# First layer of a two-layer kernel: the next chunk's score table is made from 26 rows on TensorE and six steps on VectorE

## What is computed

```python
def _L0_attn_ref(feature, wq_w, wq_b, w2_w, w2_b, ln_g, ln_b):
    q_local = feature @ wq_w + wq_b
    init_buf = feature[:, :W, :]                      # W = 64
    def step(buf, q_i):
        ki = concatenate([buf, zeros((B, 1, D))], axis=1)
        scores = einsum('bwd,d->bw', q_i[:, None, :] * ki, w2_w) + w2_b[0]
        alpha = softmax(scores, axis=1)
        v_i = einsum('bwd,bw->bd', ki, alpha)
        new_buf = concatenate([buf[:, 1:, :], v_i[:, None, :]], axis=1)
        return (new_buf, v_i)
    _, vs = lax.scan(step, init_buf, qs)              # 960 steps, one after the other
    v_local = concatenate([feature[:, :W, :], vs])
    y = tanh(v_local) * feature + feature
    return layer_norm(y, ln_g, ln_b)
x = L0_attn_feature
x = x + _layernorm(_L0_attn_ref(_layernorm(x), ...))
x = x + _layernorm(_L0_ffn_ref(_layernorm(x), ...))
```

## Time and profile before

| | |
|---|---|
| median of three runs | 2723.62 us |
| the profiled execution | 2731.38 us |
| its span | 2729.3 us |
| VectorE (DVE) busy | 2157.0 us, 79% of the span, 15955 instructions |
| ScalarE (ACT) busy | 1340.9 us, 49% |
| TensorE matmul (PE) busy | 1172.4 us, 43% |
| GpSimd (POOL) busy | 451.5 us, 17% |
| VectorE by slices of a fortieth of the span | 6999999999999999999947898866776666865233 |
| TensorE by slices | 2011010101010110101026777878877777778696 |

### The profile page before, as it was taken

How to read it: one execution, slowest core, us unless ns; L and a number is a source line. 1 busy time by engine, 2 the same in 40 slices (tenths; PEclk the granted TensorE clock), 3 DMA queues, 4 the chain that set the end, 5 groups by cost and what they waited for, 6 DMA issues and landing times. The chain is left out here.

```text
span 2729.3 us, 41936 instructions
## 1 busy us (share of the span) xinstructions
PE 1172.4 (43%) x7272; PEld 522.0 (19%) x7272; DVE 2157.0 (79%) x15955; ACT 1340.9 (49%) x3573; POOL 451.5 (17%) x1053
## 2 busy tenths in 40 slices
PE   2011010101010110101026777878877777778696
PEld 1000000000000000000011111224322333233365
DVE  6999999999999999999947898866776666865233
ACT  2343434444444434343322555658755775578642
POOL 0111111111111111111000110141024111311211
PEclk8555555555555555555566999889988988789898
DMA  5000000000000000000032031003120311001100
GB/s 144 1 4 3 5 3 5 4 4 5 3 5 3 5 3 5 3 5 5 2 79 39 1 78 32 13 16 100 24 46 19 89 44 33 22 19 35 34 1 24
DMA packets 82322, 65.85 MB, mean 24 GB/s; under 512 B 11838, under 2 KB 66920, under 8 KB 82056
## 3 DMA queue, kind: packets, MB, share of 16 engines
q1 hardware_dynamic: 78984, 56.89, 8.7%
q0 software_dynamic: 3072, 6.30, 0.7%
HBM read 34.77 MB, written 28.05 MB: 23 GB/s over the span
## 5 line engine op out<-in xcount | busy, mean ns | idle before, releaser
L1470 DVE TENSOR_REDUCE nm_half<-pair 128x2 f32<-128x1024 f32 x512 | 611.4, 1220 | 197.8 <-PE pair L1718 183.0
L342 ACT ACTIVATE ex<-row,nmax 128x65 f32<-128x65 f32 x960 | 336.1, 350 | 769.2 <-DVE row L408 676.7
L1358 ACT ACTIVATE pt<-pair 128x1024 f32<-128x1024 f32 x512 | 513.3, 1025 | 379.3 <-PE pair L1728 365.2
L403 DVE SCALAR_TENSOR_TENSOR junk<-ex,tab 128x65 f32<-128x65 f32 x2850 | 581.2, 229 | 1.9 <-issue 0.9
L523 PE MATMUL p_s<-tab,bdg 128*128 128x32 f32 x120 | 31.9, 406 | 769.2 <-DVE tab L408 769.2
L408 DVE SCALAR_TENSOR_TENSOR tab<-rz,raw 128x1 f32<-128x1 f32 (+1 forms) x1890 | 297.8, 158 | 10.9 <-ACT ex L342 5.5
L1694 PE MATMUL p_o<-pt,va 128*9 128x512 f32 x2048 | 296.1, 653 | 7.0 <-ACT pt L1358 7.0
L420 DVE STREAM_SHUFFLE row<-tab 128x130 f32<-128x130 f32 x930 | 274.8, 295 | 2.3 <-issue 2.1
L1718 PE MATMUL pair<-ks,qs 48*128 48x512 bf16 x1024 | 209.0, 419 | 112.8 <-ACT pt L1358 56.1
L403 DVE DVE_READ_ACCUMULATOR junk<-ex,tab 128x1 f32 x2850 | 233.1, 82 | 0.2
L1728 PE MATMUL pair<-qs,ks 50*128 50x512 bf16 x1024 | 210.1, 414 | 53.1 <-ACT pt L1358 23.8
(11 more groups left out here) (281 smaller groups left out, 2216.0 us busy)
## 6 DMA issues: line engine op xcount, KB each, us to landing
parts_dram<-parts SPq DMA_DIRECT2D x48, 256.0 KB, 3.5
qs<-parts_dram SPq DMA_DIRECT2D x32, 192.0 KB, 4.8
ks<-parts_dram SPq DMA_DIRECT2D x32, 192.0 KB, 5.3
hid<-xs_dram SPq DMA_DIRECT2D x33, 128.0 KB, 2.1
ys_dram<-hid SPq DMA_DIRECT2D x33, 128.0 KB, 1.8
x<-in_x SPq DMA_DIRECT2D x4, 512.0 KB, 8.5
w_W<-in_W SPq DMA_DIRECT2D x1, 2048.0 KB
w_W<-in_W SPq DMA_DIRECT2D x8, 256.0 KB
```

Source lines behind the costliest of these rows:

```text
L342: nc.scalar.activation(ex[:, r % 2, :], row[:, r % 2, 1, :], ACT.Exp, bias=nmax[:, r % 2:r % 2 + 1], accum_out=z[:, r % 2:r % 2 + 1]).then ...
L403: nc.vector.scalar_tensor_tensor(junk[:, g, :], ex[:, k, :], CAP, tab[:, g, r:r + ROW], ALU.min, ALU.mult, accum_out=raw[:, g:g + 1]).then ...
L1358: nc.scalar.activation(pt[:, kt % 2, :, tokens(t)], pair[fill.pair][:, :, :], ACT.Exp, scale=SCALE).then_inc(s_exp, 1)
L1470: nc.vector.reduce_max(nm_half[:, t, hp % 2, :, q], pair[fill.pair][:, :, :], AX.X, negate=True)\
```

## The change

`tab`'s plane 0 becomes a tensor of its own, `tab0`, with two buffers for alternate chunks and FORE = 6 more columns in front. The coefficients `tab` get two buffers too. `ex`, `z` and `rz` have four buffers instead of two, `junk` and `raw` one slot more.

In chunk c, TensorE makes the table of chunk c + 1 from the coefficients of the first FROM = 26 rows, in row 26, and no longer after row 31. VectorE reads it at the end of row 27 (`next_table`). The scores of the next chunk's queries against the last six vectors are made on VectorE as those vectors' weights come: six products over the exponentials of rows 26 to 31 (`next_products`), each followed by a division into the next column (`next_score`), placed in rows 28 to 31. Row 31 then makes the first new score of the next chunk, and rows 30 and 31 make the broadcasts for rows 0 and 1 of the next chunk, so that its row 0 follows as any other row. Only 30 rows of a chunk (SHORT) make a column of scores for the own chunk. GpSimd fills the new columns with b0 and clears the coefficients of the other buffer, behind its three copies. ScalarE's work between rows moves by one or two rows: `vr` from row 1 to 3, `vt1` from 4 to 6, `bdg` from 8-11 to 9-12, most parts of the layer norms by one row. Once, in the preparation, 16 copies of the identity are made instead of 8.

The core of the diff:

```diff
+FORE = 6
+FROM = L - FORE
+SHORT = L - 2
...
                 nc.gpsimd.tensor_copy(qn[:, :], qt[:, c + 3, :]).then_inc(s_qn, 1)
+                if c:
+                    pool.wait_ge(s_bdc, c + 1)
+                    nc.gpsimd.memset(tab[:, (c + 1) % 2, :, WIN:], 0.0).then_inc(s_clear, 1)
+                nc.gpsimd.tensor_copy(tab0[:, (c + 1) % 2, WIN:], b0_row[:, :]).then_inc(s_fill, 1)
                 applied(c)
...
-                    if r:
+                    if c or r:
                         act.sem_inc(s_pace_act, 1)
-                        act.wait_ge(s_new, (L - 1) * c + r)
...
-                    if r == 1:
+                    if r == 3:
                         act.wait_ge(s_vall, c + 1)
...
+            def products(slot, n, other, done):
+
+                nc.vector.scalar_tensor_tensor(junk[:, slot, :], ex[:, n % 4, :], CAP, other, ALU.min, ALU.mult,
+                                               accum_out=raw[:, slot:slot + 1]).then_inc(done, 1)
...
+            def next_table(c):
+
+                dve.wait_ge(s_scores, c + 2)
+                nc.vector.tensor_scalar(tab0[:, (c + 1) % 2, 0:WIN], p_s[:, 0:WIN], b0[:, :], None, ALU.add)\
+                    .then_inc(s_table, 1)
+
+            def next_products(c, i):
+
+                if i == 0:
+                    dve.wait_ge(s_fill, c + 1)
+                    dve.sem_inc(s_pace, 1)
+                    dve.wait_ge(s_table, c + 3)
+                else:
+                    dve.wait_ge(s_next, FORE * c + i)
+                products(4, FROM + i, tab0[:, (c + 1) % 2, i:i + ROW], s_raw_next)
+
+            def next_score(c, i):
+                dve.wait_ge(s_raw_next, FORE * c + i + 1)
+                divided(tab0[:, (c + 1) % 2, WIN + i:ROW + i].unsqueeze(2), 4, 5, FROM + i, s_next)
...
             for c in range(NC):
-                nc.vector.tensor_copy(tab[:, 0, WIN:], b0_row[:, :]).then_inc(s_table, 1)
-                dve.wait_ge(s_scores, c + 1)
-                nc.vector.tensor_scalar(tab[:, 0, 0:WIN], p_s[:, 0:WIN], b0[:, :], None, ALU.add).then_inc(s_table, 1)
-                dve.wait_ge(s_table, 2 * (c + 1))
-                dve.sem_inc(s_pace, 1)
-
-                nc.vector.stream_shuffle(row[:, 0, 1, :], tab[:, 0, 0:ROW], [0] * L).then_inc(s_row, 1)
-                shifted(1, 0)
-                dve.wait_ge(s_row, L * c + 1)
-                nc.vector.reduce_max(nmax[:, 0:1], row[:, 0, 1, :], AX.X, negate=True).then_inc(s_max, 1)
-                dve.wait_ge(s_bdc, c + 1)
-                nc.vector.memset(tab[:, 1:3, WIN:], 0.0).then_inc(s_clear, 1)
-                dve.wait_ge(s_clear, c + 1)
+                more = c < NC - 1
                 for r in range(L):
...
                     dve.wait_ge(s_exp, n + 1)
-                    if r:
-                        coefficients(c, r - 1)
...
+                    if n:
+                        coefficients(n - 1)
+                    nc.vector.reciprocal(rz[:, n % 4:n % 4 + 1], z[:, n % 4:n % 4 + 1]).then_inc(s_rz, 1)
+                    if more and r == L - 3:
+                        next_products(c, 1)
+                    if not final:
                         dve.wait_ge(s_row, n + 2)
...
+                        products(3, n, row[:, (n + 1) % 2, 0, :], s_raw_new)
+                    if more and r == L - 2:
+                        next_score(c, 3)
+                    if more and r == L - 1:
+                        next_products(c, 5)
+                    if r < SHORT:
+                        products(0, n, tab0[:, c % 2, FORE + r:FORE + r + ROW], s_raw_score)
+                    if not final:
+                        largest(n + 1)
+                    if more and r == L - 2:
+                        next_products(c, 4)
+                    if not final:
+                        dve.wait_ge(s_raw_new, n + 1)
                         dve.sem_inc(s_pace, 1)
                         dve.wait_ge(s_rz, n + 1)
...
+                        divided(row[:, (n + 1) % 2, 1, WIN - 1:WIN].unsqueeze(2), 3, 4, n, s_new)
+                    if more and r == L - 3:
+                        next_score(c, 1)
+                    if more and r == L - 1:
+                        next_score(c, 5)
+                    if r < SHORT:
                         dve.wait_ge(s_raw_score, m)
...
+                        divided(tab0[:, c % 2, FORE + r + WIN:FORE + r + ROW].unsqueeze(2), 0, 1, n, s_score)
+                    if more and r == L - 4:
+                        next_products(c, 0)
+                    if more and r == L - 3:
+                        next_products(c, 2)
+                    if c and not r:
+                        dve.wait_ge(s_clear, c - 1)
+                        dve.sem_inc(s_pace, 1)
+                    if n:
                         dve.wait_ge(s_coef, n)
...
+                    products(1, n, tab[:, c % 2, 0, r:r + ROW], s_raw)
+                    if more and r == L - 2:
+                        next_score(c, 4)
+                    products(2, n, tab[:, c % 2, 1, r:r + ROW], s_raw)
+                    if more and r == L - 3:
+                        next_score(c, 2)
+                    if r < SHORT:
                         dve.wait_ge(s_score, m)
                         dve.sem_inc(s_pace, 1)
...
+                        shuffled(n + 2, c, r + 2, FORE + r + 1)
+                    elif more:
+                        dve.wait_ge(s_next, FORE * c + FORE - L + 1 + r)
+                        dve.sem_inc(s_pace, 1)
+                        shuffled(n + 2, c + 1, r + 2 - L, FORE + r + 1 - L)
+                    if more and r == FROM + 1:
+                        next_table(c)
+                    if more and r == L - 4:
+                        next_score(c, 0)
+                    if more and r == L - 3:
+                        next_products(c, 3)
...
-                    nc.tensor.matmul(p_s[q, 0:L], qn[:, q], vt1[:, q], start=True, stop=True)
-                pe.wait_ge(s_coef, L * (c + 1))
+                    nc.tensor.matmul(p_s[q, 0:FORE], qn[:, q], vt2[:, L * b + FROM:L * b + L], start=True, stop=True)
+                    nc.tensor.matmul(p_s[q, FORE:FORE + L], qn[:, q], vt1[:, q], start=True, stop=True)
+                pe.wait_ge(s_coef, L * c + FROM)
                 for g in range(2):
-                    ins = nc.tensor.matmul(p_s[:, L:WIN], bdg[:, g, :], tab[:, 1 + g, WIN:], start=g == 0, stop=g == 1)
+                    ins = nc.tensor.matmul(p_s[:, FORE + L:WIN], bdg[:, g, :], tab[:, c % 2, g, WIN:WIN + FROM],
+                                           start=g == 0, stop=g == 1)
```

More of the change, by code:

```diff
@@ L70, in window_attention @@
         b0 = sb("b0", [P, 1])
-        b0_row = sb("b0_row", [P, L])
-        zero_row = sb("zero_row", [P, L])
+        b0_row = sb("b0_row", [P, FORE + L])
+        zero_row = sb("zero_row", [P, FORE + L])
         stats = sb("stats", [P, NK, 6])
@@ L85, in window_attention @@
         bdc = sb("bdc", [P, 2, P])
-        tab = sb("tab", [P, 3, WIN + L])
+        tab0 = sb("tab0", [P, 2, FORE + WIN + L])
+        tab = sb("tab", [P, 2, 2, WIN + L])
         row = sb("row", [P, 2, 2, ROW])
         nmax = sb("nmax", [P, 2])
[L91 to L95, removed]
+        ex = sb("ex", [P, 4, ROW])
+        z = sb("z", [P, 4])
+        rz = sb("rz", [P, 4])
+        junk = sb("junk", [P, 5, ROW])
+        raw = sb("raw", [P, 5])
         g_row, b_row = xt["g_row"], xt["b_row"]
@@ L395, in _ @@
                 q = slice(L * b, L * b + L)
-                for g in range(2):
-                    nc.vector.tensor_copy(tab[q, 1 + g, L * g:L * g + L], ident[q, q]).then_inc(s_init, 1)
-            dve.wait_ge(s_init, 14)
+                for u in range(2):
+                    for g in range(2):
+                        nc.vector.tensor_copy(tab[q, u, g, L * g:L * g + L], ident[q, q]).then_inc(s_init, 1)
+            dve.wait_ge(s_init, 22)
             dve.wait_ge(s_mask, 3)
-            def weighted(g, k, r, done):
-                nc.vector.scalar_tensor_tensor(junk[:, g, :], ex[:, k, :], CAP, tab[:, g, r:r + ROW], ALU.min,
-                                               ALU.mult, accum_out=raw[:, g:g + 1]).then_inc(done, 1)
@@ L419, in shifted, with shuffled @@
+            def shuffled(m, c, q, start):
+                src = tab0[:, c % 2, start:start + ROW]
                 pair = bass.AP(src.tensor, src.offset, [src.ap[0], [1, 2], [1, ROW]])
[L420 to L424, removed]
+                nc.vector.stream_shuffle(row[:, m % 2, :, :], pair, [q] * L).then_inc(s_row, 1)
@@ new lines, in _ @@
+            nc.vector.tensor_copy(tab0[:, 0, WIN:], b0_row[:, :]).then_inc(s_table, 1)
+            dve.wait_ge(s_table, 1)
+            dve.sem_inc(s_pace, 1)
+            dve.wait_ge(s_scores, 1)
+            nc.vector.tensor_scalar(tab0[:, 0, FORE:FORE + WIN], p_s[:, 0:WIN], b0[:, :], None, ALU.add)\
+                .then_inc(s_table, 1)
+            dve.wait_ge(s_table, 2)
+            dve.sem_inc(s_pace, 1)
```

(12 more changed lines are left out.)

65 lines of the change are left out of this document (29 added, 36 removed).

## The result

The changed kernel took 2694.68 us (median of four runs, 2690.15 to 2697.54) against 2724.23 us of the kernel before (four runs): ratio 0.989, 95% interval 0.987 to 0.991. Forecast were 2708 and a range from 2695 to 2722. The direction was right; the gain was -29.5 us where -15.6 was forecast, and the time lay 0.3 us under the range.

A forecast was written before the change was run, and what follows sets the result against it. VectorE and its loop through ScalarE's exponential were taken to bound the first layer, with 3.45 us per chunk boundary. Terms summed to -0.57 per boundary, -16.5 us over 29, -15.6 with preparation and last chunk: 2708 us, range 2695 to 2722.

The forecast's parts named there:

- item 1: Chunk boundary: the 3.45 us between row 31 and the next chunk's row 0 goes, -3.45 per boundary.
- item 2: Row 31 becomes an ordinary row that also makes the next chunk's first new score, +1.24 us per boundary.
- item 4: End of row 27: VectorE's read of the table moves there, without waiting for TensorE, +0.11 us per boundary.
- rival D: Matmuls come late for row 27's read or ScalarE's p_v copy, so the boundary only moves: 2724 us, chance 0.03.
- rival C: Look-ahead products and scores in rows 28 to 31 run serially, +1.40 us per boundary: 2748 us, chance 0.07.
- item 6: Row 0: GpSimd's two bdc tile products now run beside VectorE's busy row, +0.55 us per boundary, bounds 0.32 and 0.86.
- item 5: Copy of b0_row and clearing of tab move from VectorE to GpSimd, +0.08 us per boundary.
- item 7: More instructions mean more unexplained VectorE stalls, and the boundary hid its share: +0.05 us per boundary.
- items 2 to 4: Row 31 made ordinary, +1.24; six look-ahead products and scores, +0.85; table read moved to row 27, +0.11 us.
- Rival B: Contention falls where VectorE waits anyway; bdc costs 0.32, row 29's stall and extra fetches nothing: 2698 us, chance 0.22.
- Rival A: In row 0 bdc blocks VectorE for its whole 0.86 us; moved GpSimd operations cost 0.15: 2719 us, chance 0.2.
- the rule that spoke against the change: VectorE instructions with two SBUF inputs contend with GpSimd reads, the loser fully blocks; bdc's full length could be lost.

The follow-up runs named there:

- the second profile: Profile of the changed kernel, run again unchanged; its rows took 1293.2 us, against 1317.2 for the kernel before, also run again.
- the memsets: Changed kernel with eight further 128x128 GpSimd memsets per chunk, ahead of bdc: sum of row medians 42.50 us, against 42.40 without.
- the repeated run: The changed kernel once more, unchanged: 2698.25 us against 2722.51 for the kernel before, ratio 0.991.

## Why the prediction was off

The path was right: the boundary went whole (item 1), row 31 became an ordinary row (item 2), the table is there in time (item 4, rival D), the look-ahead doesn't run serially (rival C: one stall of 0.06 and one of 0.11), and the moved waits cost nothing. What failed is the size of terms of the sum, item 6 above all: bdc in row 0 was priced at 0.55 by the earlier trace rows and costs 0.39. Items 5 and 7, priced at +0.08 and +0.05, cost nothing.

| per boundary, us | forecast | measured | |
|---|---|---|---|
| items 2 to 4, rows 27 to 31 over four ordinary rows and one new | 0.96 | 1.03 | an unforeseen stall of the broadcast in row 30 |
| item 6, bdc in row 0 | 0.55 | 0.39 | shown by giving it to ScalarE |
| item 5, the moved GpSimd work | +0.08 | -0.02 | rows 1 to 7, 1.38 over ordinary rows before, 1.36 after (1.37 in the second profile) |
| item 7, stalls without a cause | +0.05 | -0.02 | mean less median: 0.85 before, 0.84 after (0.83) |
| sum with items 1 and 2 | -0.57 | -0.83 | the mean period fell by 0.90, and by 0.84 between the second profiles |

Of the 0.26, bdc is 0.16. It was taken from a pair of operations with a gap between them (starts 0.53 apart) for a pair without one (0.86 in all), whose second operation holds the one-column step for 0.12 less, as the starts and ends above show. Item 5 is 0.10: the clearing costs nothing, by the memsets, and the copy that fills the new columns cost nothing of its own either: in chunk 10 it ends at 494.61, and the coefficient step that starts at 494.58 is held until 495.04 by the layer norm's first operation, which held a product for as long before (0.30). Item 7 is 0.07; it was a guess at what is hidden in the boundary. Against these stand 0.07 too little for items 2 to 4. What the first pair's 0.90 has beyond that is mostly an ordinary row of 1.238 instead of 1.240 in the first profile of the changed kernel, 28 times a chunk; in its second the row is 1.240 again.

Rival B is nearest, and was held for the less likely, but it isn't the case that came. It had bdc at 0.32 and no stall in the look-ahead, where 0.39 and two stalls of together 0.17 were measured, and kept item 5. That its 2698 is the 2698.25 of the repeated run is partly luck. Rival A is refuted: bdc cost 0.39 of its 0.86.

29 times 0.26 is 7.5 us. The rows gained 25.8 us (24.0 in the second profile) where 16.7 was forecast, 9.1 and 7.3 more. The preparation was forecast at +1.1: from the first copy of the identity to the first reciprocal it took 2.9 us before and 3.9 after, in both pairs of profiles, so +0.9. Together the first layer gained 24.9 us, and 23.1 between the second profiles. The other 5 us of the first result are in no part of the first layer. All four executions of the changed kernel in it were of the kind with a mean granted clock of 0.70; of which kind the four of before were is not known. Of that kind alone, the eight executions of the changed kernel in both comparisons have a median of 2695.5, which is 24.8 under the 2720.3 of before. So the forecast was wrong by its terms, about 8 us; that the result fell outside the range, by 0.3 us, and not just inside it is chance. The lower end, 2695, lay 3 us under rival B, and no width was kept for the executions themselves.

On the rule that spoke against the change: a product of VectorE beside GpSimd's takes 0.48 to 0.50, up from 0.22, for an operation of 0.45. The Trainium skill (SBUF — State Buffer, Who interferes with whom) has the loser block fully, and the traces agree: a held product ends 0.08 behind the end of the GpSimd operation that it met. What the prediction made of the rule, the loss of the full length of each operation, does not follow and was not measured: VectorE lost 0.39 of 0.86, and over eight operations 0.22 to 0.23 of 0.45 each, since instructions with one input pass and a held one loses only what is left of the operation beyond its own time. That an operation of GpSimd which only writes does not contend, as the same section of the Trainium skill has it, agrees: eight memsets of 203 ns cost 0.03 to 0.10 together, and the two profiles without them differ by 0.07.

## What to carry to other kernels

Where work moves from a gap into a busy stretch, price it by what it will meet there. In this kernel a GpSimd operation that reads held the VectorE instruction with two inputs that it met until its own end: one of 0.45 us cost about 0.3 at a product met early, 0.13 at a step met late, and 0.22 to 0.23 on average over eight back to back. Where two engines pass a row back and forth, adding work to a step that is short of it costs less than its length (here 0.26 for 0.50), and taking work out of a balanced one brings little (0.06 for 0.21). Read an unchanged part of the kernel in two executions of the same code before its time is booked to the change.

## What the runs showed of the hardware

- ScalarE has room where GpSimd disturbs: four copies of 32x64 in rows 0 and 1 cost no row time, the same result by two GpSimd products 0.39 us.
- The profile's granted clock for TensorE from 100 to 1250 us reads 0.50 in some executions and 1.00 in that with bdc on ScalarE, but the 128x128 matmuls of p_v took 0.42 us in both, and the ordinary row 1.24. So these executions do not show two clocks in the first layer, and whether it matters there was not tested.
- A held VectorE instruction ends with the GpSimd operation that it met: a 65-column product 0.08 us after it, a one-column step 0.02 after it.
- VectorE sees its own results late: a product 0.19 to 0.20 us after the start of the one-column step before it, the broadcast 0.33.
